# Two residual expert layers around causal attention: first query half first, and other borders between the stages

## What is computed

```python
x = x + 0.5 * ffn(layernorm(x))
x = x + attn(layernorm(x))
x = x + 0.5 * ffn(layernorm(x))      # the same weights as the first

def ffn(x):                          # 4096 tokens, 8 experts
    logits = x @ gate_w
    top_logits, top_idx = top_k(logits, 2)
    probs = softmax of the two
    # rank of a token in its expert: first choices of all tokens count first, then the second ones;
    # those with a rank of 1280 (the capacity) or more are dropped
    h = gelu(rows_of_expert @ c_fc[e] + fc_bias[e])      # 128 -> 512
    y = h @ c_proj[e] + proj_bias[e]                     # 512 -> 128
    return sum over the token's two experts of prob * y

def attn(x):                         # 16 heads of 8, causal, softmax over keys
    q, k, v = x @ wq.T + bq, x @ wk.T + bk, x @ wv.T + bv
    return softmax(mask(q @ k.T / sqrt(8))) @ v @ wo.T + bo
```

## Time and profile before

| | us |
|---|---|
| median of 3 runs | 1066.65 (1061.44 to 1070.87) |
| the profiled execution | 1063.97 |
| its span in the profile | 1062.2 |
| TensorE busy | 843.2 (79%) |
| VectorE busy | 588.1 (55%) |
| GpSimd busy | 551.5 (52%) |
| ScalarE busy | 514.1 (48%) |

### The profile page before, as it was taken

The page is one execution under the profiler, slowest core; times in us unless marked ns, Lnnn a source line. Parts: engine busy times, 40 slices in busy tenths (PEclk is TensorE's granted clock), DMA queues, the critical chain, the costliest instruction groups (busy, mean ns, idle before and its releaser), DMA issues. The chain is left out here.

```text
span 1062.2 us, 18068 instructions
## 1 busy us (share of the span) xinstructions
PE 843.2 (79%) x6599; PEld 449.8 (42%) x6599; DVE 588.1 (55%) x1221; ACT 514.1 (48%) x836; POOL 551.5 (52%) x704
## 2 busy tenths in 40 slices
PE   8359999935778888888889888898886509999970
PEld 8237878732212323322323223332332307787850
DVE  7921212135867778877778877888770513332320
ACT  6223343402247766687556875577656204434320
POOL 5036455335444652656476564733227343777776
PEclk9869999976568999989889998998987659999995
DMA  7115565521532161431524327232101125646322
GB/s 200 71 26 142 154 205 148 189 65 50 179 86 58 27 186 34 106 77 33 169 81 109 58 46 170 83 73 58 27 2 58 35 65 119 110 70 122 48 21 20
DMA packets 101047, 95.07 MB, mean 90 GB/s; under 512 B 13835, under 2 KB 78504, under 8 KB 100968
## 3 DMA queue, kind: packets, MB, share of 16 engines
q1 hardware_dynamic: 80288, 73.39, 24.0%
q0 software_dynamic: 18688, 19.04, 11.1%
q10 hardware_dynamic: 1992, 1.60, 0.5%
HBM read 50.52 MB, written 44.50 MB: 89 GB/s over the span
## 5 line engine op out<-in xcount | busy, mean ns | idle before, releaser
L1808 DVE TENSOR_REDUCE m_blk<-banks 128x8 f32<-128x1024 f32 (+1 forms) x320 | 349.9, 1114 | 90.4 <-PE banks L1428 59.8
L1732 ACT ACTIVATE pt<-banks 128x1024 f32<-128x1024 f32 (+3 forms) x384 | 299.0, 810 | 153.4 <-PE banks L1412 151.9
L1462 PE MATMUL banks<-pt,vs 128*32 128x512 f32 (+3 forms) x1536 | 178.7, 540 | 8.5 <-POOL pt L2153 7.6
L2153 POOL TENSOR_SCALAR_AFFINE_SELECT pt<-pt 128x512 f32<-128x512 f32 x128 | 81.7, 640 | 186.0 <-ACT pt L1732 185.6
L1412 PE MATMUL banks<-qb,kp 64*128 64x512 bf16 (+3 forms) x768 | 136.9, 357 | 46.3 <-DVE m_blk L1808 38.0
L635 POOL DMA_INDIRECT out_dram<-ys,ids x80 | 124.2, 1553 | 67.9 <-issue 32.9
L1428 PE MATMUL banks<-kp,qa 64*128 64x128 bf16 (+4 forms) x1152 | 128.7, 297 | 28.4 <-DVE m_blk L1808 16.3
L801 POOL DMA_INDIRECT xe<-xn_rows,slot_tok x80 | 80.0, 1000 | 99.0 <-PE banks L1141 39.2
L1428 PEld LDWEIGHTS banks<-kp,qa 48*128 48x128 bf16 (+1 forms) x1152 | 46.2, 98 | 141.7 <-ACT pt L1732 101.7
L1058 ACT ACTIVATE he<-banks,b_up 128x512 f32<-128x512 f32 (+1 forms) x96 | 57.9, 616 | 87.5 <-PE banks L1141 87.3
L1412 PEld LDWEIGHTS banks<-qb,kp 64*128 64x128 bf16 x768 | 37.2, 95 | 148.9 <-DVE m_blk L1808 85.8
(11 more groups left out here) (329 smaller groups left out, 945.3 us busy)
## 6 DMA issues: line engine op xcount, KB each, us to landing
bucket<-zero SPq DMA_DIRECT2D x16, 660.0 KB
qb<-q_stack SPq DMA_DIRECT2D x32, 192.0 KB, 3.4
qa<-q_stack SPq DMA_DIRECT2D x30, 192.0 KB, 3.7
kp<-k_stack SPq DMA_DIRECT2D x30, 192.0 KB, 4.6
xb<-bucket SPq DMA_DIRECT2D x8, 660.0 KB, 5.0
q_stack<-qp SPq DMA_DIRECT2D x18, 256.0 KB
k_stack<-kq SPq DMA_DIRECT2D x18, 256.0 KB
y_slots<-ye SPq DMA_DIRECT2D x16, 256.0 KB, 2.6
```

The lines of the kernel that those rows point to most:

```text
L1462: i = nc.tensor.matmul(o_bank[VW * h:VW * h + VW, q:q + w], vs[par][:, kb, h, :], pt[u % PTS][:, h, 0:w], start=u in (0, turn_at), stop=u ...
L1732: nc.scalar.activation(pt[u % PTS][:, 2 * pair:2 * pair + 2, 0:w], ring[SLOT["score", 2 * u + pair]][:, :, 0:w], ACT.Exp, scale=SCALE).the ...
L1808: nc.vector.tensor_reduce(dst, ring[slot][:, :, 0:blocks * P].rearrange("p s (j k) -> p s j k", k=P), AX.X, ALU.max).then_inc(m_done, 1)
L2153: nc.gpsimd.affine_select(out=v, in_=v, compare_op=ALU.is_ge, fill=0.0, base=0, pattern=[[0, HS], [1, P]], channel_multiplier=-1).then_inc ...
```

## The change

**Slot table.** For each half of the tokens the large product `a_tok` is made ahead of the 32 `b_one`, and these are counted in fours (`B_STEP`), so that the products can begin before all are there.

**First expert layer.** Chunks of 2, 4 and 4 tiles (`CHUNKS1`).

**Prologue.** The first query half's maxima (6 pieces) come first, two of them ahead of the projections of the second tokens' half. `move` of the first half stands ahead of the stores of heads 8 to 15; those of the keys go from ScalarE to SP, behind it. The clearing of `kp` and `vs` goes from VectorE to ScalarE.

**Groups.** Every group takes its first query half first; the second half's maxima are split and moved in unit 0, the next group's first half at its end. `M_IN_UNIT` is new. In the last group of batches 1 and 2 GpSimd's scatters stay in units 0 to 3, where the masks of the first half now stand. The gathers of a batch after the last one, whose result nothing used, are gone.

**Last group.** Only the 8 scatters of the second tokens' half are left in it, in units 4 to 7; the other 8 come after it. The addition of the output bias goes from GpSimd to VectorE.

**Late router and change of stage.** The ranks of the first half no longer stand behind the output projection; they have a bank of PSUM of their own (`late_bank`). The weights of experts 0 and 1 are loaded during the late router, and the rows of expert 0 before the stage changes, into tiles that the attention stage has done with.

**Second expert layer.** The sends are plain writes: a token's row for its first choice goes to one half of a table `y_tab`, that for its second choice to the other, and rows of expert 7 to a table `y_last`. The tables are cleared in each batch's group 0 by three stores of 512 KB. x after attention goes to `mid`, not to the output. At the end SP loads it and the tables by quarters, VectorE adds them and ScalarE stores the output.

```diff
-    UNITS = [(1, k) for k in range(T)] + [(0, k) for k in range(T // 2)]
+    UNITS = [(0, k) for k in range(T // 2)] + [(1, k) for k in range(T)]
...
-    M_IN_UNIT = [2, 2, 2, 2, 2, 2, 2, 1, 2, 1, 1, 1]
+    M_IN_UNIT = [2, 2, 1, 1, 2, 2, 2, 2, 2, 2, 2, 0]
...
-    TAIL = ["r_t0", ("ctx1", NG - 1), "r_lg0", "o_t1", "o_p1", "r_rk0", "r_t1", "r_lg1", "r_rk1"]
+    TAIL = ["r_t0", "r_lg0", ("ctx1", NG - 1), "r_rk0", "o_t1", "o_p1", "r_t1", "r_lg1", "r_rk1"]
...
+    y_tab = nc.dram_tensor("y_tab", [TOPK * N, D], f32, kind="Internal").ap()
+    y_last = nc.dram_tensor("y_last", [N, D], f32, kind="Internal").ap()
...
+        CHUNKS1 = [(0, CT - 8), (CT - 8, 4), (CT - 4, 4)]
...
+                    load_rows(1, 1, row_of(window, 1))
+                    for i in range(B):
+                        sp.dma_start(acc[i][:], by_rows(mid, 0, i)).then_inc(acc_ld, 16)
+                    with nc.sync.Fori(1, E // 2) as h:
+                        load(h, 0)
+                        load(h, 1)
+                    sp.wait_ge(sent[0], 16 * CT * (E // 2))
+                    sp.wait_ge(sent[1], 16 * CT * (E // 2 - 1))
+                    for i in range(B):
+                        for k in range(TOPK):
+                            sp.dma_start(tab[k][i][:], by_rows(y_tab, k * N, i)).then_inc(quarter_ld[i], 16)
+                    sp.wait_ge(sent_last, 16 * CT)
+                    for i in range(B):
+                        sp.wait_ge(sum_tab, i + 1)
+                        sp.dma_start(tab_l[i][:], by_rows(y_last, 0, i)).then_inc(quarter_ld[i], 16)
...
+                        wait(dve, sent[q], 16 * CT * use)
...
+                        on = 0.0 if last else float(N)
+                        nc.vector.tensor_scalar(ti[:], xb[q][:, :, C_ID], SKIP - on, None, ALU.subtract)
...
+                    def send(e, q, table, rows_of, done):
                         for cc, (t0, n) in enumerate(CHUNKS):
                             wait_apart(pool, y_ready, NC * e + cc + 1)
                             for t in range(t0, t0 + n):
                                 nc.gpsimd.indirect_dma_start(
-                                    dest, bass.IndirectOffsetOnAxis(ap=ids[q][:, t:t + 1], axis=0), ys[q][:, t, :],
-                                    None, bounds_check=N - 1, oob_is_err=False, compute_op=ALU.add).then_inc(added, 16)
-                    pairs(nc.gpsimd, E // 2, send)
-                    wait_apart(pool, added, E * CT * 16)
+                                    table[:, :], bass.IndirectOffsetOnAxis(ap=ids[q][:, t:t + 1], axis=0), ys[q][:, t, :],
+                                    None, bounds_check=rows_of - 1, oob_is_err=False).then_inc(done, 16)
+                    send(0, 0, y_tab, TOPK * N, sent[0])
+                    send(1, 1, y_tab, TOPK * N, sent[1])
+                    with nc.gpsimd.Fori(1, E // 2 - 1) as h:
+                        send(2 * h, 0, y_tab, TOPK * N, sent[0])
+                        send(2 * h + 1, 1, y_tab, TOPK * N, sent[1])
+                    send(E - 2, 0, y_tab, TOPK * N, sent[0])
+                    send(E - 1, 1, y_last, N, sent_last)
+                    pool.wait_ge(sent[0], 16 * CT * (E // 2))
+                    pool.wait_ge(sent[1], 16 * CT * (E // 2 - 1))
+                    pool.wait_ge(sent_last, 16 * CT)
...
+                    nc.vector.tensor_scalar(a_tok[c][:, :, :, 0, :], a_one[c][:], pid[:], None,
+                                            ALU.mult).then_inc(b_hot, 1)
                     for t in range(U):
                         for k in range(TOPK):
                             i = nc.vector.tensor_scalar(b_one[c][:, t, k, :], iota_low[:], low_f[:, t, k:k + 1], None,
                                                         ALU.is_equal)
-                    i.then_inc(b_hot, 1)
-                    dve.wait_ge(a_eq, c + 1)
-                    nc.vector.tensor_scalar(a_tok[c][:, :, :, 0, :], a_one[c][:], pid[:], None,
-                                            ALU.mult).then_inc(b_hot, 1)
...
                 def table(c):
-                    pe.wait_ge(b_hot, 2 * c + 2)
-                    pe.wait_ge(a_num, c + 1)
-                    for k in range(TOPK):
-                        for t in range(U):
+                    for t in range(U):
+                        if t % B_STEP == 0:
+                            pe.wait_ge(b_hot, (U // B_STEP + 1) * c + t // B_STEP + 2)
+                        pe.wait_ge(a_num, c * U + t + 1)
+                        for k in range(TOPK):
...
+                    if g == 0:
+                        for table, row in ((y_tab, 0), (y_tab, N), (y_last, 0)):
+                            sp.dma_start(by_rows(table, row, b), zero[:, 0:T * D].rearrange("p (t d) -> p t d", d=D)
+                                         ).then_inc(tab_zero, 16)
...
                 load_k(0, 1)
+                move(pro_at[("max1", 0)], 0, 0, 0, 0)
                 store_pieces(sp, 0, 2 * HS, NH, stack_st)
-                move(pro_at[("max1", 0)], 1, 0, 0, 0)
+                store_pieces(sp, 1, 2 * HS, NH, stack_st)
                 sp.wait_ge(stack_st, STORES)
...
+                wait_apart(sp, c_evac, LAST_NORM + 1)
+                ws = ((xnT[:], early_b[0]), (xn[:].rearrange("p t d -> p (t d)"), early_b[1]))
+                for e, (w, b_dn) in enumerate(ws):
+                    expert_weights(sp, e, early_up(w), early_down(w), b_dn[:], w_ld2[e])
                 store_x2(tail_at, b)
+                sp.wait_ge(win2, WINDOW_STEPS)
+                at = row_of(window, 0)
+                sp.wait_ge(scattered[0], 16 * TOPK * T * B)
+                sp.dma_start(early_rows(gy), bucket_rows(at)).then_inc(rows_ld2[0], 16)
                 wait_apart(sp, x2_st, 16 * B)
+                sp.wait_ge(tab_zero, 16 * 3 * B)
...
+                norm_task(pro_at, "x_t1", 0)
+                for m in range(PAIRS):
+                    first_maxima(m)
+                norm_task(pro_at, "q1", 0)
+                norm_task(pro_at, "k1", 0)
+                pe.wait_ge(c_evac, pro_at["q1"] + 1)
                 for j in range(3):
                     stack_parts(1, 0, j)
-                for m in range(NM):
-                    wait(pe, m_done, m - 2)
-                    if m < PAIRS:
-                        pe.wait_ge(st_evac, 2 * PAIRS + m + 1)
-                    maxima(0, 0, m, m % 3)
-                    if m == 1:
+                for m in range(PAIRS, NM):
+                    first_maxima(m)
+                    if m in (3, 5):
                         pe.wait_ge(c_evac, pro_at["k1"] + 1)
                         for j in range(3):
-                            stack_parts(1, 1, j)
-                    if m == 3:
+                            stack_parts(1, 1, j, [(m - 3) // 2])
+                    if m == 7:
                         pe.wait_ge(st_evac, 4 * PAIRS)
                         norm_task(pro_at, "v1", 0)
-                    if m == NM1 + 2:
+                    if m == NM1 + 3:
                         max_rows_of(pro_at[("max1", 0)], 0, 0)
...
+                for t_ in kp[1:]:
+                    i = nc.scalar.copy(t_[:].rearrange("p i (t k) -> p (i t) k", k=P),
+                                       k_edge[:, None, :].broadcast_to([P, HS // 2 * T, P]))
+                i.then_inc(kp_clear, 1)
...
-                store_pieces(act, 1, 2 * HS, NH, stack_st)
-                take_max(pro_at[("max1", 0)], 0, 1)
+                take_max(pro_at[("max1", 0)], 0, 0)
...
+                        if is_last(b, g) and u == 5:
+                            dve.wait_ge(x2_ld, 16 * (b + 1))
+                            nc.vector.tensor_tensor(x2[:], x2[:], bo_r[:, None, :].broadcast_to([P, T, D]),
+                                                    ALU.add).then_inc(x2_bias, 1)
...
+                late_rank(0, step0)
                 add_out(tail_at, "o_p1", b)
                 late_moments(1, tail_at["o_p1"])
-                late_rank(0, step0)
...
+                FIRST_HALF, SECOND_HALF = ([k * T + t for k in range(TOPK) for t in range(T) if t // HB == half]
+                                           for half in range(2))
+                LAST_TURNS = [0, 0, 0, 0, 1, 3, 5, 7, 8, 8, 8, 8, 8]
...
+                        if u == NU - 1 and more:
+                            split_max(n + 1, 1, 2 * n + 3, at[("max1", g + 1)] + 1)
+                        if u in MASKED:
                             mask(n, u)
...
+                            if is_last(b, g):
+                                turns = SECOND_HALF[LAST_TURNS[u]:LAST_TURNS[u + 1]]
+                            else:
+                                turns = range(3 * u, 3 * u + 3) if u < 4 else range(u + 8, min(u + 9, TOPK * T))
...
+                for k in FIRST_HALF:
+                    router_scatter(pool, 0, k)
                 late_rstd(1)
```

315 lines of the change are left out of this document (170 added, 145 removed).

## The result

The changed kernel takes 1037.49 us (median of 4 runs, 1034.86 to 1038.5) beside 1068.76 (4 runs) of the kernel before: a ratio of 0.9715, 95% interval 0.966 to 0.9769. It is faster by some 2.9%. The prediction was 1038, range 1020 to 1055.

What follows compares the result with a forecast made beforehand. TensorE was taken as first bound, VectorE second, with a final tail that is GpSimd's alone. Gains summing to 27.9 us gave a call of 1036.1; adding 2.7 for the median gave 1038.8, stated as 1038, range 1020 to 1055.

Steps and rivals of the forecast that it cites:

- First expert layer: First layer's chunks: earlier first transposes, partly given back to the slow clock, plus a smaller last store; gain 1.6 us.
- Into attention: Border to attention: first scores 3.8 us earlier, then a wait at the first group's unit 4; net gain 0.6 us.
- Loss 3.2: First group, unit 4: second half's rows, queued behind twelve stores on SP, land late; loss 3.2 us.
- The groups: Ordinary attention groups: better spread gains 4.5 us, scatters among masks in two groups cost 5; sum a loss of 0.5.
- 0.3 us per group for the better spread: Ordinary attention groups: the new distribution of maxima over units gains 0.3 us in each of 15 groups, 4.5 together.
- Last group: Last attention group: only eight scatters left, in units without masks, and bias addition on VectorE; gain 6 us.
- Late router and handover: Into the second expert layer: late scatters end 1.5 us earlier, rows load beside the change of stage; together 6.5 gain.
- The tail: After the second layer's last result: plain sends into tables, then loads and additions, end at T + 23; gain 10.6 us.
- Six sends remain, to T + 6.5: End of second expert layer: after the last result, at T, six plain sends of 1.29 us remain, ending at T + 6.5.
- (a): Attention groups get slower: POOL's work or second-half rows late at unit 3 or 4; chance 0.12 slight, 0.05 strong.
- (c): Tail and handover give little: transfers collide or the early load must wait; 10 of 17 us lost, 1049; chance 0.10.
- (b): Attention groups: spread works better, TensorE's idle time falls by half with fewer clock drops; 30 us more, 1008; chance 0.15.

Runs made afterwards that it cites:

- after_again: The changed kernel run once more, unaltered, in a job with three variants: 1036.18 us, ratio 0.9752 to the kernel before.
- add_sends: Changed kernel with sends adding into the output again, each expert's waiting for the previous landing; no tables, clears or final sums: 1041.52 us, ratio 0.9769.
- gathers: Changed kernel with the 16 unused gathers of batch 2 put back in groups 1 and 2: 1036.36 us, ratio 0.9733.
- early_move: Changed kernel with the prologue's second-half move right behind the twelve stores, ahead of the wait for their landing and two loads: 1026.29 us, ratio 0.9643.
- oldspread: Changed kernel with the units of maxima spread over the group as in the kernel before: 1027.79 us, ratio 0.9624.
- best2: Changed kernel with maxima spread as before, the prologue's second-half move ahead of the waits, and final additions into x after the last sends: 1024.73 us, ratio 0.9606.
- adds_late: Changed kernel with VectorE's four final additions into x waiting until the last expert's sends have landed: 1036.47 us, ratio 0.9714.
- groups_only: Kernel before with only the new order of groups, prologue and late router, weights still loaded early: 1057.45 us, ratio 0.9938.
- clears_end: Changed kernel with the twelve table-clearing stores moved from groups 0 to SP's work in the last group: 1030.52 us over 6 runs, ratio 0.966.

## Why the prediction was right or wrong

The forecast of 1038 was met, but partly by luck: two of its terms were off by 4.3 and 8.0 us and cancelled.

- **Slot table: right.** 16.1 to 13.0 us from the second `a_one` to the first gather, the 3.1 of the sum.
- **First expert layer: sign right, size off.** Two gathers fewer gave 2.6. But the sum let the slow clock take back only 0.6 of it. The clock rose at the same moment in both profiles, 74.8, so that the early start was worked off at 1.2 GHz. First the kernel before, then the changed one, from its first transposes to that moment:

```profile
66.90:74.80 7.90, 6.76 (x11) 3.24 (x12) 0.76 (x2) 2.73 (x4) 4.99 (x5) 0.50 0.23 50
```

```profile
61.80:74.80 13.00, 10.64 (x20) 5.72 (x21) 1.19 (x3) 4.33 (x7) 6.92 (x7) 0.50 0.19 42
```

  In executions of the changed kernel and its variants whose clock rose earlier behind the transposes (5.6 us instead of 12.9 in `after_again`) the layer took 156.0 (`after_again`, `add_sends`, `gathers`), so the two steps together give 3 to 6 us beside the one profile of the kernel before.
- **Into attention: the mechanism right, one term mis-sized.** The first scores gained 4.4 (3.8 predicted). The hole at unit 4 was forecast, in its place and with its cause, at 3.2; it was 5.0, because the move also stood behind the wait for the stores' landing (2.5 us) and two loads, while the stores themselves took 0.70 us each to issue and not 0.93. The step that failed is "Loss 3.2": it priced the wait and not the clock, which fell in the wait and stayed low for 17.1 us. `early_move` shows 9.5 us between the same groups with and without it; with the old spread, where the clock had not risen before the wait, the difference is 1.7 (`oldspread`, `best2`).
- **The groups: the scatters right, the sum wrong.** The loss by scatters among masks was 2.8 us of waits in one of the two groups and 1.1 in the other (2.5 each predicted), and the second half's rows were in time in all 14 groups of this profile; `gathers` shows that the margin can go. But "0.3 us per group for the better spread" found no support: waits grew from 60.0 to 65.7, and with the old spread put back the kernel did not get slower (`oldspread`). Whether the old spread is the better one is open: alone it was 8.7 us shorter than `adds_late`, but on top of the early move it gave nothing clear of noise (ratios 0.9606 and 0.9643, with overlapping intervals). The 7.5 us gained came from TensorE's clock (0.93 to 0.95), which the text had only as the bound of the term. `groups_only` has it too, without the changes around the groups; why this order is granted more is not shown.
- **Last group: right** (5.3 of 6). Its masks now come 1.1 to 1.6 apart, and 32.7 came back in `groups_only`.
- **Late router and handover: right** (1.8 of 1.5; 4.3 of 5.0). The change of stage on TensorE is what is late next; with rows loaded after it the handover took 14.3.
- **The tail: right in kind, 2.8 short in this pair.** "Six sends remain, to T + 6.5" was 10.9, since additions and sends hinder each other; the end was at T + 25.8 instead of T + 23. The last table's first piece was there 4.0 us after its issue (4.5 was taken), which gave a little back. Against adding sends in the same kernel the tail with tables is 9.8 shorter, since that tail is 35.6 and not 33.6, but the whole by only 5. The prediction's upper bound for this term doesn't follow from the price that it names: pieces at 3.2 instead of 4.5 make it 11.9 and not 15; and in the lower one six sends at 1.85 instead of 1.29 cost 3.4 and not 3.0. The section that it quotes for 3.2 us (the Trainium skill, DMA: Bandwidth & Descriptors, Anatomy of one DMA) is on DMAs that GpSimd issues; these loads are SP's, and their 4.0 lies between that estimate and the row's 5.2.
- **Rivals.** (a) and (c) didn't occur in this pair. (b) came with its 7.5 in the groups, a quarter of what it put up, but by clock and without fewer waits. A wait for the rows at unit 4 of an ordinary group, as (a) has it, was seen once, in the profile of `gathers`.

So 1038 was met with two errors of opposite sign, 4.3 too little loss in the first group and 8.0 too little gain in the others, beside 1.7 and 2.8 too much gain elsewhere. The sum gave 1036.1 for the profiled call, which took 1038.4. The 2.7 that it added for the distance of the median did not come (the median is 0.9 below the profiled call), and this too brought the forecast near.

## What to carry to other kernels

When a transfer is moved ahead in a queue, list what the *next* one of its kind then stands behind, the waits for landing among them; here one move placed a few lines earlier gave 10 us, a third of what the whole change had. Price a hole in TensorE's work by its length and, in a second sum, by the clock after it: here 5.0 us of waiting stood for 9.5 in one pair of profiles, and 4.1 for 1.7 in another, where the clock was low in any case. And where a stretch gets shorter, ask the busy time and the clock first: here a better spread seemed to have worked, and putting the old one back cost nothing.

## What the runs showed of the hardware

- A signal that GpSimd gives behind an indirect transfer in its program came before that transfer's work was done (additions tied to it began 5.5 us ahead of the end of the last send); additions tied to the transfers' own semaphore began behind it (`adds_late`: 1020.38, the last send ends at 1019.16).
- A plain indirect send took 0.97 us alone, 0.97 beside a VectorE addition with one operand in PSUM, and 1.41 to 1.97 when it began during the last additions, with both in SBUF. One that adds in DRAM took 1.56 (mean of 80 in `add_sends`).
- The granted clock rose to 2.4 GHz at 300.0, TensorE then stood still for 5.0 us, and from 303.4 on it was 1.2 GHz for 17.1 us (changed kernel, first group).
- Executions of one kernel differ by up to 15 us (1026.4 to 1041.2 in `clears_end`) while nearly all groups repeat within 0.1 us. Of the 9.3 us between the profiles of the changed kernel (spans 1036.6 and 1027.3) 4.4 lie ahead of the second `a_one`, 3.0 in the first expert layer and 1.8 in the first group.
